# Cross-attention and expert feed-forward: products ahead of the second count, two-tensor steps with an operand in PSUM, the probabilities on VectorE

## What is computed

```python
logits = xn @ router_weight.T + router_bias
probs = jax.nn.softmax(logits, axis=-1)
_, idx = jax.lax.top_k(logits.T, top_k)          # top_k = 512 per expert
xe = xn[idx]
h = jax.nn.gelu(einsum('ecd,efd->ecf', xe, fc1_weight) + fc1_bias[:, None, :], approximate=False)
y = einsum('ecf,edf->ecd', h, fc2_weight) + fc2_bias[:, None, :]
gates = take_along_axis(probs.T, idx, axis=1)
output = zeros.at[flat_idx].add((y * gates[:, :, None]).reshape(-1, d))
gate_sums = zeros.at[flat_idx].add(gates.reshape(-1, 1))
output = where(gate_sums > 0, output / gate_sums, output)
```

## Times and profile before

| | us |
|---|---|
| runs of the kernel before, median (lowest, highest) | 1036.74 (1033.07, 1045.97), 3 runs |
| the profiled execution, its own time | 1034.88 |
| the span that its trace covers | 1033.2 |
| busy in that span: PE / DVE / POOL / ACT | 880.7 / 772.4 / 591.3 / 519.1 |

### The profile page before, as it was taken

The page is one execution under the profiler, slowest core; times in us unless marked ns, Lnnn a source line. Parts: engine busy times, 40 slices in busy tenths (PEclk is TensorE's granted clock), DMA queues, the critical chain, the costliest instruction groups (busy, mean ns, idle before and its releaser), DMA issues. The chain is left out here.

```text
span 1033.2 us, 20448 instructions
## 1 busy us (share of the span) xinstructions
PE 880.7 (85%) x6051; PEld 698.3 (68%) x6051; DVE 772.4 (75%) x1691; ACT 519.1 (50%) x951; POOL 591.3 (57%) x566
## 2 busy tenths in 40 slices
PE   3889999999999999999851116999999999999995
PEld 2556766776676677667440115888888888899985
DVE  4668878878887888888448876798777877777742
ACT  1455565556556555655415502654554655565531
POOL 3246656556565655656553135646787677775435
PEclk9889999999999999999855556999999999999998
DMA  4345555655555565555331105336766556665433
GB/s 146 133 155 184 203 196 182 225 187 190 209 191 205 183 224 188 192 208 197 115 132 54 41 18 146 107 118 181 170 166 172 148 154 173 176 155 132 128 67 41
DMA packets 110062, 159.95 MB, mean 155 GB/s; under 512 B 19380, under 2 KB 76980, under 8 KB 109896
## 3 DMA queue, kind: packets, MB, share of 16 engines
q1 hardware_dynamic: 94408, 133.78, 37.7%
q0 software_dynamic: 15616, 25.70, 12.0%
HBM read 66.55 MB, written 26.28 MB: 90 GB/s over the span
## 5 line engine op out<-in xcount | busy, mean ns | idle before, releaser
L532 DVE TENSOR_REDUCE NM<-bank 128x4 f32<-128x480 f32 x256 | 159.7, 656 | 53.7 <-PE bank L642 53.4
L375 ACT ACTIVATE PT<-bank 120x512 f32<-120x512 f32 x256 | 139.0, 595 | 66.4 <-PE bank L667 65.6
L316 POOL TENSOR_SCALAR XN<-X,mv,rstd 128x256 f32<-128x256 f32 x128 | 155.3, 1221 | 6.9 <-POOL rstd L311 6.1
L1556 PE MATMUL bank<-W2H,HH 128*128 128x256 f32 x512 | 144.8, 283 | 2.0 <-issue 2.0
L1558 PE MATMUL bank<-W2H,HL 128*128 128x256 f32 x512 | 143.8, 281 | 0.4 <-issue 0.4
L1557 PE MATMUL bank<-W2L,HH 128*128 128x256 f32 x512 | 143.6, 280 | 0.0
L991 POOL DMA_INDIRECT out_dram<-C,IO x60 | 110.1, 1836 | 53.9 <-issue 30.9
L1280 DVE TENSOR_TENSOR HL<-hf,HH 128x512 fp32r<-128x512 f32 x128 | 87.1, 690 | 43.6 <-ACT HH L1435 35.9
L642 PEld LDWEIGHTS bank<-KX,QX 128*128 128x128 f32 x512 | 71.8, 192 | 61.3 <-issue 28.7
L485 DVE RECIPROCAL RR<-RC 128x256 f32<-128x256 f32 x64 | 111.3, 1741 | 1.5 <-DMA RC<-PVS 1.5
L349 POOL TENSOR_TENSOR XB<-X,bp_sb 128x512 f32<-128x512 f32 x32 | 40.5, 1265 | 124.3 <-DVE X L543 124.3
(11 more groups left out here) (184 smaller groups left out, 1858.4 us busy)
## 6 DMA issues: line engine op xcount, KB each, us to landing
QX<-QH SPq DMA_DIRECT2D x64, 256.0 KB
W<-w1T_dram SPq DMA_DIRECT2D x16, 1024.0 KB
W<-w2T_dram SPq DMA_DIRECT2D x16, 1024.0 KB
KX<-KH SPq DMA_DIRECT2D x64, 240.0 KB, 2.3
X<-x_dram SPq DMA_DIRECT2D x32, 256.0 KB, 2.8
QX<-QL SPq DMA_DIRECT2D x32, 256.0 KB
RC<-PVS SPq DMA_DIRECT2D x32, 256.0 KB, 2.4
OC<-PVS SPq DMA_DIRECT2D x32, 256.0 KB, 2.6
```

The costliest lines, as they stand in the source:

```text
L316: ins = pool.tensor_scalar(dst[:, t, :], src[:, t, :], mv[:, t, 0:1], rstd[:, t:t + 1], ALU.subtract, ALU.mult)
L375: act.activation(PT[u][0:M, HE * k:HE * (k + 1), :], score_bank[k % 2][0:M, :], ACT.Exp, scale=SCALE) \
L532: dve.tensor_reduce(NM[u][:, t, :].rearrange("p (f n e) -> p n e f", n=HN, e=HE)[:, n, :, :], smax_bank[q % 2][:, 0:4 * M].rearrange("p (e ...
L1556: pe.matmul(o, wh, xh, start=first, stop=False)
```

## The change

There are five edits, all in `routed_phase`.

1. Small tiles move to PSUM, into bank 2 that the search used: `rsm` and `gate_scale`, and a new one, `tails`, into which the last numbers of the tiles are copied out of `prefix` ahead of the first `spread_of`. Three two-tensor products that had both operands in SBUF (both calls of `spread_of`, and the product that makes `gates`) now have one in PSUM.
2. `probs` is made on DVE behind the second `spread_of`, and no longer on POOL; the reciprocal ahead of it moves there too, from the end of the search.
3. `chosen` is the difference of neighbouring values of `prefix`: a one-column minimum, a one-column subtraction and a subtraction of 1023 columns take the place of two steps over 1024 columns.
4. On DVE `columns(0, 0)` stands ahead of `find_first(1)`.
5. PE's unread products: 6 where 3 were ahead of the transposes of `XG[0]`, and 12 where 5 were behind them.

```diff
+    tails, rsm, gate_scale = (cnt_bank[:, 64 * k:64 * (k + 1)].rearrange("p (t o) -> p t o", o=1) for k in range(1, 4))
@@ gpsimd @@
-        pool.wait_ge(rsm_ready, 1)
-        pool.tensor_tensor(probs[:, :, :], expl, rsm[:, :, :].to_broadcast([P, NT, E]), ALU.mult).then_inc(probs_ready, 1)
@@ vector @@
-        dve.wait_ge(sum_ready, 4)
-        dve.reciprocal(rsm[:, :, :], tree[3]).then_inc(rsm_ready, 1)
...
-                              prefix[:, P - 1:CT:P].rearrange("p (a b j) -> p a b j", a=1, b=1).to_broadcast([P, hi - lo, NC, TC]),
+                              tails[:, 0:TC, :].rearrange("p (a j) b -> p a b j", a=1).to_broadcast([P, hi - lo, NC, TC]),
...
-            dve.reciprocal(gate_scale[:, :, :], gate_sum[:, :, :]).then_inc(gate_step, 1)
+            dve.reciprocal(gate_scale, gate_sum[:, :, :]).then_inc(gate_step, 1)
...
+        then(dve.tensor_copy(tails[:, 0:TC, 0], prefix[:, P - 1:CT:P]))
         spread_of(0, 2)
...
         tiles(0)
-        then(dve.scalar_tensor_tensor(eq, eq_count, need[:, 4:5], eq, ALU.is_le, ALU.mult))
-        dve.tensor_tensor(chosen, gt, eq, ALU.add).then_inc(chosen_ready, 1)
+        then(dve.tensor_scalar(need[:, 6:7], need[:, 5:6], need[:, 4:5], None, ALU.min))
+        dve.tensor_tensor(chosen[:, 0:1], prefix[:, 0:1], need[:, 6:7], ALU.subtract)
+        dve.tensor_tensor(chosen[:, 1:CT], prefix[:, 1:CT], prefix[:, 0:CT - 1], ALU.subtract).then_inc(chosen_ready, 1)
         spread_of(2, E)
+        dve.wait_ge(sum_ready, 4)
+        dve.reciprocal(rsm, tree[3]).then_inc(rsm_ready, 1)
+        dve.wait_ge(rsm_ready, 1)
+        dve.tensor_tensor(probs[:, :, :], expl, rsm.to_broadcast([P, NT, E]), ALU.mult).then_inc(probs_ready, 1)
         find_first(0)
         gate_values()
...
         dve.wait_ge(c_loaded, 32)
+        columns(0, 0)
         find_first(1)
-        columns(0, 0)
@@ tensor @@
-        keep_clock(3)
+        keep_clock(6)
         columns(0, 0, True)
-        keep_clock(5)
+        keep_clock(12)
         up(0, 0, range(5), True)
```

More of the change, by code:

```diff
@@ L826, in routed_phase @@
     out_row = sb("out_row", [P, E, GT], I32)
-    gate_total, no_gate, gate_sum, gate_scale = (sb(n, [P, NT, 1], FP32) for n in
-                                                 ("gate_total", "no_gate", "gate_sum", "gate_scale"))
+    gate_total, no_gate, gate_sum = (sb(n, [P, NT, 1], FP32) for n in
+                                                 ("gate_total", "no_gate", "gate_sum"))
     B2 = pair("B2", [P, D], FP32)
@@ L859, in routed_phase @@
                                     for u in range(2) for v in range(2))
-    mx, rsm = gate_total, no_gate
+    mx = gate_total
     LT = hf4[:, 0:2, :].rearrange("p n s -> p (n s)")
@@ L1192, in gate_values @@
             dve.wait_ge(gate_step, 4)
-            dve.reciprocal(gate_scale[:, :, :], gate_sum[:, :, :]).then_inc(gate_step, 1)
+            dve.reciprocal(gate_scale, gate_sum[:, :, :]).then_inc(gate_step, 1)
             dve.wait_ge(gate_step, 5)
             dve.tensor_tensor(gates.rearrange("p j (c e) -> p c j e", e=E), probs[:, :, :].rearrange("p (c j) e -> p c j e", j=TC),
-                              gate_scale[:, :, :].rearrange("p (c j) o -> p c j o", j=TC).to_broadcast([P, NC, TC, E]),
+                              gate_scale.rearrange("p (c j) o -> p c j o", j=TC).to_broadcast([P, NC, TC, E]),
                               ALU.mult).then_inc(gates_ready, 1)
```

## The result

The changed kernel took 1045.12 us in the median of 20 runs (1040.06 to 1051.18), the kernel before 1042.07 in the median of 20 (1033.07 to 1048.22). The ratio is 1.0046 with a 95% interval of 1.0025 to 1.0067: 4.8 us slower, between 2.6 and 7.0. The two medians lie 3.05 apart, inside that interval. The time forecast was 1037.9 with a range to 1042.0, so the measured one lies outside it. The profiled execution of the changed kernel took 1044.16, its span is 1042.4.

What follows compares the result with a forecast made beforehand. POOL's serial chain from the landing of gather 1 to the gather of expert 2 was taken to decide; gather 1 +1.3 and the chain's half-clock +0.8 gave +2.1 us on 1035.8: 1037.9, range 1032.5 to 1042.

Steps and rivals of the forecast that it cites:

- The base: Time of the kernel before, taken as 1035.8, midway between the profiled execution's 1034.88 and a median 1.9 above it.
- The mechanism: First product 2.3 us sooner, but gather 1 later; PE's gain goes into a wait at expert 2; sum +2.1 us.
- gather 1: POOL's gather behind the second count: issued 1.9 us later at 633.1, landed in 3.5 at 640.35, 1.3 later.
- The search's end: Reciprocal leaves the path, copy into `tails` joins it: net -0.35 to -0.55 us, taken as -0.4.
- First transfer of ranks: On POOL, meets DVE's new subtraction; starts at 609.56 and ends at 611.1, 0.25 us sooner.
- First columns on PE: PE's transposes of `XG[0]` behind the gates and six unread products start at 627.5 for 627.63.
- Expert 2: Gather of expert 2 comes 1.3 us later at 668.6, PE arrives at 664.3 and waits 4.3 us.
- 667.25 beside 667.30 leaves no slack: Before the change, gather of expert 2 and PE arrive together, so a later gather delays PE at once.
- Expert 4: POOL's chain reaches PE's transposes of expert 4 at 718.6, PE at 718.55, for 716.47 before; +2.1 us.
- The clock at expert 2: PE's wait exceeds the 2.0 us after which its clock fell; half clock costs PE 2.7, the chain 0.8.
- The gain stays: Rival: gather 1 lands as before or POOL's chain shortens, so part of -2.3 to -3.0 gets through; 1033.2; 15%.
- The PSUM operand frees nothing: Rival: POOL's second transfer again over 2 us, only -0.4 remains, gather 1 lands 2.4 later; +3.2, 1039.0; 15%.

Runs made afterwards that it cites:

- e4: The changed kernel with `tails` and `gate_scale` in SBUF instead of PSUM; one execution, 1042.76 us.
- e9: The changed kernel with SP's 1 MB load of expert 3's first weight issued only after the gather of expert 2 landed; 0.9981 of the kernel before.
- e12: The kernel before, unchanged, profiled a second time; one execution, 1047.7 us.
- e6: The kernel before with one edit alone, 6 and 12 unread products for 3 and 5; 1.0031 of the kernel before.
- e5: The changed kernel with the old order of count and columns and the old 3 and 5 unread products; 0.9997 of the kernel before.
- e1: The changed kernel with `find_first(1)` put back ahead of `columns(0, 0)` on DVE; 0.9957 of the kernel before.

## Why the prediction was right and wrong

**The base.** "I put the kernel before at the middle of the two, 1035.8" is the step that put the time outside the range. Twenty runs have their median at 1042.07, 6.3 above. Of the 7.2 us between the 1045.12 measured and the 1037.9 forecast, 6.3 are this. The profile that was read was of one of the fastest executions. As far as two profiles of that kernel show, two things made it so: POOL's chain met none of the delays of its added rows (8.0 us of the 12.8 between the two), and the search ended early (4.8; over all the profiles of this study it ended 1.5 later on average). The runs shown reached to 1045.97, and that was read as noise to be put into the range instead of as a sign that the profile might sit at one end.

**The mechanism.** That the first product starts sooner and the kernel is still slower, because gather 1 is issued later and PE's gain goes into a wait at expert 2, was right. The forecast had 2.1 us slower; measured are 4.8 (2.6 to 7.0). The 2.9 us by which the profiles place expert 2 later lie in that interval; what the rest is, the runs do not say. The steps, from the search, forecast and measured in the profiles:

- The search's end: the transfers start 0.3 sooner (0.4 forecast). The copy took 0.17, the small spread 0.29 for 0.38.
- First transfer of ranks: it took 1.64 where the forecast had 1.54 (609.56 to 611.1), and ended where it had (0.25 sooner forecast), 1.11 behind the subtraction. The second 0.97, as forecast, for another reason (e4). `XG[0]` starts 1.2 sooner (1.6), its last transfer ends 2.2 sooner (2.6).
- First columns on PE 0.1 later (0.1 sooner forecast). But "the transposes then take 0.8 to 1.6; I take `xt_done` at 628.5" assumed a clock that rises 4.6 us behind PE's start. It rose after 5.5, so the six products and most of the transposes ran at half clock, and `XTH` started 1.4 sooner and not 2.3. The first product is 1.4 sooner, not 2.3.
- That same lateness goes on into gather 1, issued 2.7 later and not 1.9, since the count stands behind the columns. It then landed in 2.9 and not 3.5, 1.6 later from the search (1.3 forecast). PE waited 0.9 for it and not 2.0, and started expert 1 2.9 sooner (3.0 forecast): that this came out is luck, since the issue was 0.8 later than forecast and the landing 0.6 quicker.
- Expert 2: 2.9 later, forecast 1.3. It is the 1.6 of gather 1, 0.3 more up to the start of the last transfer, and 1.8 in its landing, less 0.7 of slack that I had not seen. "667.25 beside 667.30 leaves no slack" was a misreading: where PE and POOL's next row wait for the same gather of expert 2, 3 or 4, POOL starts 0.67 to 0.77 us behind PE (672.48 and 673.16 here, 716.47 and 717.15 in the kernel before). So before the change that gather was there for PE at about 666.6, and PE came 0.7 late. "POOL's chain then gives the gather of expert 2 at 667.30 + 1.3" took the landing of that gather for constant, at the 3.7 to POOL's next row. It was 5.5, since SP's load now came ahead of its last transfer. PE, ACT and DVE had become earlier while the gather had become later, and so the load moved past it. That step moved a load past a queue, and I had not looked at it. e9 shows it.
- Expert 4: 5.9 later by the profiles, forecast 2.1. Expert 3 was 3.4 later; 2.6 came at the added rows of expert 0, whose last transfer took 2.35 for 1.57 and which were waited for 5.91 for 4.11. Both kernels have such delays in some executions (2.92 and 5.88 in e12), so this part is not to be put down to the change.

**The clock at expert 2.** I had it fall 2.0 us into the wait. It stayed full for some 5.2 us of idling and then was down for less than 4 us. The cost was forecast as 0.8 in the chain and 2.7 in PE's work. From the transposes of expert 2 to those of expert 3, waits left out, PE took 25.0 us for 23.5, 1.5 more; no run tests it by itself. Ahead of the first product the clock held, as forecast. But e12 held it too without the added products, and e6 lost it with them, so the part of the gain put down to them is not shown.

**The rivals.** "The gain stays" did not happen. e5 has no gain even with an earlier gather 1, and e1 a small one (0.9957 by the ratio, 0.9984 by the medians). "The PSUM operand frees nothing" was half true: nothing at the spread, 1.05 at the gates. In the sum the second transfer came out right for the wrong reason. Its way of telling, a second transfer over 2 us, would have named the wrong cause.

## What to carry to other kernels

Before a single profile is taken as the base of a sum, look at where in the spread of the timed runs it lies, and look for serial chains of transfers whose waits could be longer than this profile has them. When a change makes one side earlier and another later, ask which transfers of other queues then pass each other. A wait for a landing ahead of the next issue is worth taking away where the data allow it: here two of them cost some 11 us, more than all five edits moved.

## What the runs showed of the hardware

- Three indirect transfers of POOL that started inside a DVE step with two SBUF operands ended 0.82 to 0.85 us behind that step (two of before, one of e4), and the first of a row in the changed kernel 1.11 behind; beside PSUM and SBUF operands one took 0.94.
- A two-tensor step over 896 columns took 1.69 us with an operand read at every 128th column (before), and 1.08 with a dense one, in SBUF (e4) as in PSUM (changed).
- POOL went on 3.5 to 4.3 us behind the start of the last transfer of the gather of expert 2 when no 1 MB load of SP was issued until 2.2 us or more behind that start (seven profiles), and 5.5 to 6.6 us behind it when one was issued ahead of the start or 0.17 behind it (six profiles).
- When PE and POOL's next row waited for the same gather (experts 2 to 4, 30 cases in the 16 profiles), PE started 0.67 to 0.77 us ahead of POOL.
- PE's granted clock fell to 0.50 2.0 us into a gap of 3.3 us in one execution and did not fall in the same gap in another. It held for some 5.2 us of a third gap, and in e6 it fell half a microsecond after PE had started again. It came back 3 to 5.5 us behind a start of PE.
